# RWKV block in a fused four-layer kernel: feed-forward mixed rows and the second mixing sum on GpSimd, whose receptance product goes behind its gating product

## The reference, cut to what matters

```python
xa = ln(x, ln1_w, ln1_b)
sx = concat([state[:, 1:2] - xa[:, :1], xa[:, :-1] - xa[:, 1:]], axis=1)
xxx = tanh((xa + sx * maa_x) @ maa_w1).reshape(b, l, 5, DM)
xxx = einsum('blfd,fde->blfe', xxx, maa_w2)
xm = xa[:, :, None] + sx[:, :, None] * (maa_stack + xxx)      # 5 mixed rows
xk, xw, xv, xr, xg = (xm[:, :, j] for j in range(5))
w = exp(-exp(time_decay + tanh(xw @ td_w1) @ td_w2))
r, k, v, g = xr @ Wr.T, xk @ Wk.T, xv @ Wv.T, silu(xg @ Wg.T)
# scan over tokens: out = r (u*k*v + s); s = k*v + w*s
x1 = x + (group_norm(out) * g) @ Wo.T
xc = ln(x1, ln2_w, ln2_b)
sx2 = concat([state[:, 0:1] - xc[:, :1], xc[:, :-1] - xc[:, 1:]], axis=1)
xk2, xr2 = xc + sx2 * ffn_maa_k, xc + sx2 * ffn_maa_r
return x1 + sigmoid(xr2 @ Wfr.T) * (square(relu(xk2 @ Wfk.T)) @ Wfv.T)
```

## Time and profile before

| | us |
|---|---|
| median of 3 runs (982.54 to 985.4) | 982.9 |
| span of the profiled execution | 982.8 |
| PE busy (x8321) | 944.6 |
| DVE busy (x974) | 592.1 |
| ACT busy (x1026) | 462.5 |
| POOL busy (x572) | 411.8 |

### The profile page before, as it was taken

One profiled execution on the slowest core, in us unless ns is written; L12 is line 12 of the kernel. 1 busy time (PEld: TensorE's weight loads), 2 busy tenths in 40 slices (PEclk: granted clock), 3 DMA queues, 4 the chain that ended last, 5 costly groups with the idle time before them and its releaser, 6 DMA issues.

```text
span 982.8 us, 21494 instructions
## 1 busy us (share of the span) xinstructions
PE 944.6 (96%) x8321; PEld 795.7 (81%) x8321; DVE 592.1 (60%) x974; ACT 462.5 (47%) x1026; POOL 411.8 (42%) x572
## 2 busy tenths in 40 slices
PE   6999999989999999999999999999999999999998
PEld 4777777966788888988897888998888888678776
DVE  5899986767544433344356433344426766999883
ACT  4677874237643333333334333333342434576565
POOL 2143346875365333333246343342422862344231
PEclk9999999999999999999999999999999999999999
DMA  9100000310011110111101110111100100000000
GB/s 298 37 23 2 2 2 22 116 54 2 1 55 50 54 50 25 37 54 48 54 7 55 50 54 21 42 49 48 54 22 18 41 14 1 1 2 6 13 6 23
DMA packets 24147, 37.15 MB, mean 38 GB/s; under 512 B 4432, under 2 KB 16528, under 8 KB 23824
## 3 DMA queue, kind: packets, MB, share of 16 engines
q1 hardware_dynamic: 24080, 36.23, 11.9%
HBM read 35.17 MB, written 1.05 MB: 37 GB/s over the span
## 4 chain that ended last, share of the span: by engine, by line
PE 74%; DVE 12%; ACT 5%; issue 4%; POOL 4%; DMA 0%; DVEq 0%; ACTq 0%; POOLq 0%
PE ps L1292 18%; PE ps L790 13%; PE ps L1309 9%; PE ps L1351 6%; PE ps L1948 5%; PE ps L890 4%; PE ps L1327 4%; PE ps L1337 2%; DVE sb L2476 2%; DVE sb L656 1%; PE ps L270 1%; DVE sb L650 1%; PE ps L2026 1%; PE ps L421 1%; PE ps L2112 1%
## 5 line engine op out<-in xcount | busy, mean ns | idle before, releaser
L837 POOL TENSOR_TENSOR sb<-sb 128x256 fp32r<-128x256 f32 (+1 forms) x128 | 102.5, 801 | 278.0 <-DMA sb<-in_heads_a 144.9
L1292 PE MATMUL ps<-sb 128*128 128x512 f32 x768 | 187.7, 396 | 1.0 <-issue 1.0
L1292 PEld LDWEIGHTS ps<-sb 128*128 128x128 f32 x768 | 139.5, 188 | 33.0 <-ACT sb L1425 3.1
L790 PE MATMUL ps<-sb 128*128 128x256 f32 x1152 | 148.4, 286 | 0.0
L790 PEld LDWEIGHTS ps<-sb 128*128 128x128 f32 x1152 | 141.4, 191 | 2.1 <-issue 0.2
L839 POOL TENSOR_TENSOR sb<-sb 128x256 fp32r<-128x256 f32 (+1 forms) x128 | 115.8, 905 | 10.0
L1522 DVE SCALAR_TENSOR_TENSOR sb<-ps,sb 128x512 fp32r<-128x512 f32 x64 | 45.1, 747 | 95.6 <-ACT sb L1458 95.5
L1309 PE MATMUL ps<-sb 128*128 128x256 f32 x768 | 99.2, 285 | 0.4 <-DVE sb L1490 0.4
L1502 DVE TENSOR_REDUCE sb<-ps 128x8 f32<-128x520 f32 x32 | 22.4, 700 | 126.6 <-PE ps L1327 126.6
L1309 PEld LDWEIGHTS ps<-sb 128*128 128x128 f32 x768 | 95.0, 191 | 3.0 <-issue 0.9
L1425 ACT ACTIVATE sb<-ps,sb 128x512 f32<-128x512 f32 x64 | 43.8, 685 | 107.9 <-PE ps L1292 107.8
(11 more groups left out here) (221 smaller groups left out, 1668.2 us busy)
## 6 DMA issues: line engine op xcount, KB each, us to landing
sb<-in_heads_a SPq DMA_DIRECT2D x32, 386.0 KB, 3.0
sb<-in_heads_c SPq DMA_DIRECT2D x16, 256.0 KB, 3.6
sb<-in_heads_b SPq DMA_DIRECT2D x32, 128.0 KB, 3.1
sb<-in_mlp_a SPq DMA_DIRECT2D x16, 128.5 KB, 2.1
sb<-in_mlp_b SPq DMA_DIRECT2D x16, 128.0 KB, 2.1
sb<-in_w_r SPq DMA_DIRECT2D x1, 2048.0 KB, 7.5
sb<-in_encT SPq DMA_DIRECT2D x1, 1024.0 KB, 6.2
sb<-in_ctx SPq DMA_DIRECT2D x1, 1024.0 KB, 8.1
```

The costliest lines, as they stand in the source:

```text
L790: last = pe.matmul(m.acc(t), lhsT[x], rhs[w], start=opens and n == 0, stop=False, skip_group_check=True)
L837: pool.tensor_tensor(high, src, one, ALU.mult).then_inc(*G.did(name + "_high", u))
L1292: last = pe.matmul(m.ps[u][:, c, :], m.w_parts[u][w][:, (KD * q + k) * P:(KD * q + k + 1) * P], rows[x][:, k, c * 512:(c + 1) * 512], star ...
```

## The change

Weights are no longer prepared for the feed-forward part: four of POOL's five 512- and 256-column instructions in `rwkv_consts_gpsimd` go. Instead the rows are mixed for each tile: sx2 (256 columns), sx2 times both factors (512 columns), plus xc (512 columns), into a double buffer `m.xkr` (signal "xkr"). POOL does it for tiles 0 to 5 as the last step of its slot, DVE for tiles 6 and 7 in its tail. `ffn_keys` becomes 4 products of 128x128, `ffn_receive` 2 products of 128x256 with 128 weight columns. `mix2` moves from DVE to POOL, right behind `first`, and POOL's `gated` (the gating product) moves ahead of `receive` (the receptance product) and `f_state`. xc is free for the next tile once it is mixed.

```diff
-    pool.tensor_tensor(m.wfks, m.wr[:, W_FK, :, :], wide("ffn_k", D), ALU.mult)
-    pool.tensor_tensor(m.wfrs, m.wr[:, W_FR, :, :], wide("ffn_r", D), ALU.mult)
     pool.tensor_tensor(m.headsum_u, bc(m.headsum[:, :], 1, [P, KD, P]), wide("u", P), ALU.mult).then_inc(m.s_scaled, 1)
-    pool.wait_ge(m.s_scaled, 1)
-    pool.tensor_tensor(m.wr[:, W_FK, :, :], m.wr[:, W_FK, :, :], m.wfks, ALU.subtract)
-    pool.tensor_tensor(m.wr[:, W_FR, :, :], m.wr[:, W_FR, :, :], m.wfrs, ALU.subtract).then_inc(m.s_scaled, 1)
...
-    ffn_parts = [(m.wr[:, W_FK, :, :], m.wr[:, W_FR, :, :], k, 1) for k in range(KD)]\
-        + [(m.wfks, m.wfrs, k, 0) for k in range(KD)]
-
     @of_tile
     def ffn_keys(i):
-        pe.wait_ge(*done["xc"].at(i))
-        pe.wait_ge(*done["f_state"].at(i))
+        pe.wait_ge(*done["xkr"].at(i))
         for e in range(KD):
             last = product(m.key_bank(i)[:, e * P:(e + 1) * P],
-                           [(wk[:, k, e * P:(e + 1) * P], m.xc[:, k, :, s:s + S]) for wk, _, k, s in ffn_parts])
+                           [(m.wr[:, W_FK, k, e * P:(e + 1) * P], m.xkr[i % 2][:, 0, k, :]) for k in range(KD)])
         last.then_inc(*done["kk_raw"].did(i))
...
-        for n, (_, wr, k, s) in enumerate(ffn_parts):
-            for b in range(2):
-                last = pe.matmul(m.receive_bank(i)[b * S:(b + 1) * S, D:2 * D], m.xc[:, k, b, s:s + S], wr[:, k, :],
-                                 start=n == 0, stop=n == len(ffn_parts) - 1)
-        last.then_inc(*done["kk_rr"].did(i))
+        product(m.receive_bank(i)[:, D:2 * D],
+                [(m.xkr[i % 2][:, 1, k, :], m.wr[:, W_FR, k, :]) for k in range(KD)]).then_inc(*done["kk_rr"].did(i))
...
     def ffn_rows(i):
         act.wait_ge(*done["f_turned"].at(i))
         if i >= 1:
-            act.wait_ge(*done["kk_rr"].at(i - 1))
+
+            act.wait_ge(*done["xkr"].at(i - 1))
...
-    def mix2(i):
-        xm = m.xm[i % 2].rearrange("p f (n s) -> p f n s", s=S)
-        xa = m.xa[i % 2].rearrange("p k b s -> p (k b) s")[:, :, 1:S + 1]
-        vec.wait_ge(*done["mixed"].at(i))
-        vec.tensor_tensor(xm, xm, bc(xa, 1, [P, ND, 4, S]), ALU.add).then_inc(*done["xm"].did(i))
...
+    def ffn_mix(i):
+
+        rows = m.xc[:, :, :, :].rearrange("p k b s -> p (k b) s")
+        split = lambda x: x.rearrange("p (b s) -> p b s", b=2)
+        vec.wait_ge(*done["xc"].at(i))
+        vec.wait_ge(*done["f_state"].at(i))
+        if i == BY_VECTOR[0]:
+            vec.wait_ge(*done["xkr"].at(i - 1))
+        vec.tensor_tensor(m.sx2.rearrange("p k (b s) -> p (k b) s", b=2), rows[:, :, 0:S], rows[:, :, 1:S + 1],
+                          ALU.subtract).then_inc(*m.own_vec.did("sx2", i))
+        vec.wait_ge(*m.own_vec.at("sx2", i))
+        vec.wait_ge(*done["kk_rr"].at(i - 2))
+        for f, name in enumerate(("ffn_k", "ffn_r")):
+            for k in range(KD):
+                last = vec.scalar_tensor_tensor(out=split(m.xkr[i % 2][:, f, k, :]), in0=split(m.sx2[:, k, :]),
+                                                scalar=m.col(name, k), in1=m.xc[:, k, :, 1:S + 1], op0=ALU.mult,
+                                                op1=ALU.add)
+        last.then_inc(*done["xkr"].did(i))
...
+    ffn_mix(LAST - 1)
     attended(LAST)
-    for i in (LAST - 2, LAST - 1, LAST):
+    ffn(LAST - 2)
+    close(LAST - 2)
+    ffn_mix(LAST)
+    for i in (LAST - 1, LAST):
         ffn(i)
...
+    def mix2(i):
+        xm = m.xm[i % 2].rearrange("p f (n s) -> p f n s", s=S)
+        xa = m.xa[i % 2].rearrange("p k b s -> p (k b) s")[:, :, 1:S + 1]
+        pool.wait_ge(*done["mixed"].at(i))
+        pool.tensor_tensor(xm, xm, bc(xa, 1, [P, ND, 4, S]), ALU.add).then_inc(*done["xm"].did(i))
...
     def f_state(i):
         if i >= 1:
-            pool.wait_ge(*done["kk_rr"].at(i - 1))
+
+            pool.wait_ge(*done["xkr"].at(i - 1))
         pool.tensor_copy(m.xc[:, :, :, 0], state(i, 0)).then_inc(*done["f_state"].did(i))
+
+    def ffn_mix(i):
+
+        rows = m.xc[:, :, :, :].rearrange("p k b s -> p (k b) s")
+        pool.wait_ge(*done["xc"].at(i))
+        pool.wait_ge(*done["f_state"].at(i))
+        pool.tensor_tensor(m.sx2.rearrange("p k (b s) -> p (k b) s", b=2), rows[:, :, 0:S], rows[:, :, 1:S + 1],
+                           ALU.subtract).then_inc(*m.own_pool.did("sx2", i))
+        pool.wait_ge(*m.own_pool.at("sx2", i))
+        if i >= 2:
+            pool.wait_ge(*done["kk_rr"].at(i - 2))
+        factors = m.colbuf[:, COL["ffn_k"]:COL["ffn_k"] + 2 * KD].rearrange("p (f k) -> p f k", f=2)
+        pool.tensor_tensor(m.xkr[i % 2], bc(m.sx2, 1, [P, 2, KD, P]), bc(factors, 3, [P, 2, KD, P]), ALU.mult)\
+            .then_inc(*m.own_pool.did("sxf", i))
+        pool.wait_ge(*m.own_pool.at("sxf", i))
+        mixed = m.xkr[i % 2].rearrange("p f k (b s) -> p f (k b) s", b=2)
+        pool.tensor_tensor(mixed, mixed, bc(rows[:, :, 1:S + 1], 1, [P, 2, 4, S]), ALU.add)\
+            .then_inc(*done["xkr"].did(i))
+
+    @of_tile
+    def ffn_mix_early(i):
+        if i not in BY_VECTOR:
+            ffn_mix(i)
...
         first(slot - 4)
+        mix2(slot - 3)
+        gated(slot - 5)
         receive(slot - 4)
         f_state(slot - 6)
-        gated(slot - 5)
         bonus(slot - 3)
+        ffn_mix_early(slot - 6)
 
...
-        m.wfks, m.wfrs, m.headsum_u = (
-            scaled(at, n) for at, n in ((0, D), (KD * D, D), (KD * 2 * D, P)))
+        m.xkr = [consts[:, at:at + 2 * D].rearrange("p (f k n) -> p f k n", f=2, k=KD) for at in (0, KD * D)]
+        m.headsum_u = scaled(KD * 2 * D, P)
+        m.sx2 = scaled(KD * (2 * D + 3 * P), P)
```

More of the change, by code:

```diff
@@ L1913 @@
 LONE = range(LAST - 3, TILES)
+BY_VECTOR = range(LAST - 1, TILES)
 TILE_SIGNALS = ("a_state", "xa", "lora", "xx", "mixes", "mixed", "xm", "td1", "td", "td2", "rkvg", "rkv", "tanh",
@@ L2436, in mix2 @@
     @of_tile
-    def mix2(i):
-        xm = m.xm[i % 2].rearrange("p f (n s) -> p f n s", s=S)
-        xa = m.xa[i % 2].rearrange("p k b s -> p (k b) s")[:, :, 1:S + 1]
-        vec.wait_ge(*done["mixed"].at(i))
-        vec.tensor_tensor(xm, xm, bc(xa, 1, [P, ND, 4, S]), ALU.add).then_inc(*done["xm"].did(i))
-    @of_tile
     def gate(i):
@@ L2559, in rwkv_vector @@
         out_heads(slot - 6)
-        mix2(slot - 4)
         if slot == 4:
@@ L2876, in build @@
         m.tile_done["kk_raw"] = Signal(m.done["ctx_ps"].sem, len(ITEMS))
+        m.tile_done["xkr"] = Signal(m.done["ctx"].sem, len(ITEMS))
         m.own_vec, m.own_act, m.own_pool = (Own(sem(n)) for n in ("vector_own", "scalar_own", "gpsimd_own"))
@@ L3012, in _ @@
             mlp_tensor(pe, ph["mlp2"], m, 12, HALVES[:-LATE])
-            rwkv_tensor(pe, m, ph["mlp2"], 12, [(m.s_scaled, 2)])
+            rwkv_tensor(pe, m, ph["mlp2"], 12, [(m.s_scaled, 1)])
 def lay_out(inputs):
```

## The result

The changed kernel takes 995.6 us (median of 4 runs, 994.78 to 996.52) against 983.07 for the kernel before (4 runs, 982.54 to 985.4): a ratio of 1.0114, 95% interval 1.0094 to 1.0135, so it is slower, by 12.5 us between these medians and by 11.2 us by the ratio. The forecast was 993. The profiled execution took 996.24 us, 0.6 above the median, with a span of 994.4 and a mean granted clock of 0.986.

A forecast was written before the change was run, and what follows sets the result against it. PE bounds the steady laps, with DVE and POOL's shared SBUF read as second resource; single steps set the tail. 3.7 + 1.4 + 5.2 + 0.4 - 0.5 = 10.2 us on 982.8 gave 993, range 980 to 998.

The forecast's parts named there:

- the shared read: DVE and POOL: when both read SBUF twice they exclude each other, making a second resource beside PE's 18.75 us.
- PE's part: Keys and receive on PE: fewer instructions save 1.9 us a tile, so a PE-bound lap would be 16.9 us.
- POOL's new instructions: On POOL: mix2 takes 2.9 us (cheapest 2.3), ffn_mix 3.2 us (between 2.9 and 3.5).
- The lap: Three laps from project(4) to project(7): 19.9, 18.7, 18.6 us against 18.75, 18.76, 18.38, so +1.3.
- faster rival: No exclusion, or POOL's work falls in DVE's free stretches; laps 16.9 to 17.2 us, total 979; chance 0.18.
- The way up: Tiles ahead of project(4): longer wait for mix2 and a late tile 3, +2.4 us at project(4), ends 0 and +4.
- The tail: After project(7): three steps, +1.4 (rest of step one), +5.2, and +0.4 with -0.5.
- Step one: Tail: POOL's bonus(7), ffn_mix(4) and f_rstd(5) stand ahead of first(7), which scan0(7) needs; scan0(7) at 957.3, +5.1 us.
- Step two: Tail: PE's keys(5), ahead of gather(7), waits for POOL's ffn_mix(5); 11.6 us behind group_norm(6) instead of 6.4, +5.2.
- Step three: Tail's end: ffn_mix(6) ahead of attended(7) +0.4 us; ffn_mix(7), shorter keys and receive(7) moved, -0.5 in all.
- much slower: Rival: PE idles up to 3 us a lap and the clock falls, some 3 us each lap: 1002; chance 0.10.
- No change: Rival: way up gains what laps lose, ffn_mix(5) done before PE reaches keys(5): about 984 us; chance 0.12.

The follow-up runs named there:

- e2: The changed kernel with mix2 back on DVE, ffn_mix and the order gated, receive kept as changed; 989.8 us, ratio 1.0057 to the kernel before.
- e10: Changed kernel with mix2 on DVE, keys(5) behind center(7), f_rstd(5) ahead of ffn_mix(4), ffn_mix(5) on DVE, ffn_mix(6) behind attended(7); 985.61 us, 1.0014.
- e11: e10 with ACT's f_normed(6), square(7) and std(7) ahead of relu(5) and relu_square(5); 982.74 us, ratio 0.9995 to the kernel before.
- e3: The changed kernel with POOL's gated behind receive and f_state again; 999.41 us, ratio 1.0143 to the kernel before.
- e6: The kernel before with a useless POOL addition of 1280 columns, both inputs in SBUF, per tile behind first; 990.04 us, ratio 1.0063.
- e7: The kernel before with a useless POOL memset of 2048 columns, reading nothing, per tile behind first; 984.35 us, ratio 1.0000.
- e1: The changed kernel with PE's keys(5) moved behind gather(7) and center(7); 991.36 us, ratio 1.0062 to the kernel before.

## Why the prediction was right, step by step

**The total and the sign** held: 995.6 against 993, in the range. That the total came so near is luck. I had project(7) 3.7 us late and the tail 6.5 us longer, 10.2 in all. Measured in the profiled executions, project(7) is 0.6 us late, of which 1.4 belongs to the run, so the change's own part is 0.7 us *sooner*; and the tail is 11.0 us longer. The change's own sum is 10.3, from an error of 4.4 us one way and one of 4.5 the other. The sign rests on the tail alone. Both mechanisms are seen, the shared read and keys(5), but the first one costs mix2's 4.6 us against e2 and does not make the laps longer than before.

**PE's part** (1.9 us saved a tile, a PE-bound lap of 16.9): right; e2 shows laps of 17.2, 17.2 and 16.9, with PE busy 16.7, 16.7 and 16.3.

**POOL's new instructions**: mix2 measured 2.68 us (2.9 taken, 2.3 the low end), and ffn_mix 3.18 at the place shown (914.37 to 917.55; 3.2). Right for ffn_mix, 0.2 too much for mix2.

**The lap** is the first term that failed. Its mechanism held (project waits for POOL's mix2, shift is stretched to its end, the scans alternate with gated and receive), but I added up +1.3 us over three laps and they came out 1.8 shorter than before (54.1 us from project(4) to project(7) for 55.9; predicted 57.2). Step by step in the lap of project(5), from the end of mix2(5) at 903.90: (1) shift to group_norm ends at 907.22 for 3.46 taken, 3.3; (2) scan1, gated and receive to 912.32, 5.1 for 5.5; (3) DVE's receive and bonus to 914.37, 2.05 for 2.1; (4) to 917.55, 3.2; (5) to 918.95, 1.4 for 1.28 and hand-overs of 0.2; (6) 2.68 for 2.9. That is 17.7 where I had 18.7: many small excesses, all on one side. It lies as near to the 16.9 to 17.2 of the faster rival as to my figure, but with shift stretched to 2.25 us and project waiting for mix2, which that rival rules out. I had priced each turn at full durations although the waiting instruction's start-up goes on during the wait: shift ended 0.28 us behind mix2, not its own 0.41.

**The way up** (+2.4 at project(4), ends 0 and +4): project(4) came 2.4 us later, but 1.4 of that was there before the changed code (2.56 at project(0), less the 1.2 of a longer mix2(0)). The change's own part is about 1.1 us, where I had 1.0 beyond mix2(0). The late project(3) is there; what I did not have is that it takes 5.25 us for the 3.81 before, at a granted clock of 0.82 from 860 to 868, behind a wait of 1.85 us; these 1.4 us alone would cover the 1.1. In the sum of the low ends there is a slip: 0.8 us a lap, 1 in the tail and 2.4 on the way up make 5.8, not some 7, so that bound is 987; the range that was stated reaches down to 980 and does not hang on it.

**The tail** is the second: counted from project(7) its steps measured 1.8, 6.7 and 2.5 us for the 1.4, 5.2 and -0.1 predicted. Step one had scan0(7) at 957.3 from first(7); it was at 954.55, and not first(7) held it but f_rstd(5), through f_normed(5), square(6) and group_sum(6). The POOL queue that I followed was the right one, the instruction in it that mattered was another: I had only asked what stands ahead of first(7), not who waits for what stands beside it. Step two, keys(5) waiting for ffn_mix(5) with gather(7) behind it, is seen as predicted: from the end of group_norm(6), 956.67 + 0.42, to L2052 at 969.66 are 12.6 us for 11.6 predicted and 6.4 before. The clock covers the difference: keys took 2.08 us where 0.9 was taken. bonus(7) is 9.1 us late (10.3 predicted). Step three was undersized: from bonus(7) to the end it is 23.0 us after and 20.5 before, +2.5, where I had -0.1. The last sixteen matmul rows alone took 5.49 us where they take 3.21 at full clock (e10, e11), 2.3 of the 2.6 us that this step lacked.

**The clock** was my "much slower" rival, with a place in the laps. It did not fall in the three laps (1.00 in the lap shown), but on the way up at project(3), in the laps of e3 (0.53 behind a wait of 2.44 us), and in the tail, where PE now waits: 0.50 through the last sixteen rows and through keys(5) behind its gap of 5.15 us. I had noted that the tail before kept 1.00 in spite of 4.4 us of gaps, and took that for granted with the 16.2 us that the same part has now (27.23 us busy of 43.40). With some 4 us it is most of what the tail's sum lacked.

**The rivals.** "Faster" falls with e6 and e7. "No change" would have needed gather(7) free of keys(5); e1, where it is, is still 1.0062. e11 is near zero, but with mix2 back on DVE besides, which is worth 4.6 us by itself. "Much slower" came true in size only in part and in another place.

The rule of the Trainium skill that the prediction cites (SBUF — State Buffer, Who interferes with whom) has a DVE instruction with two SBUF inputs contend with a GpSimd one that reads SBUF, not with one that only writes it. By that rule e6 and e7 come out as they did: 2042 ns for mix2 beside the addition, 1483 beside the memset, 1482 before. By the occupancy rule in the Trainium skill's Perfetto Trace Analysis (Identifying the Most-Contended Engine) POOL at 12.3 of 17.7 us busy would still have room. Project waited 1.12 us for POOL in that lap; here the measurement decides against that rule.
